# First batch of a fused graph kernel: one copy moved to ScalarE's queue, one message moved behind the distances, and a small addition moved from VectorE to GpSimd near the end

## The reference

```
h = relu(bn(conv1(x)));  x_conv = relu(bn(conv2_17taps(h)) + x)
s = x @ w_se.T + b_se                       # 3 numbers per node
A = exp(-(|s_n|^2 + |s_m|^2 - 2 s_n.s_m)) * adj
x_nmp = A @ relu(x @ w_msg.T + b_msg)
r, z, n = gates([x_conv, x_nmp] @ w_ih.T, x @ w_hh.T);  x = layernorm(x + (1-z)*n + z*x)
# per group g of the first 25 nodes:
A = adj_g + eye;  dinv = deg(A) ** -0.5
out_g = relu((dinv*A*dinv) @ relu((dinv*A*dinv) @ x @ W1[g] + b1[g]) @ W2[g] + b2[g])
```

## Time and profile before

| | |
|---|---|
| median of 3 runs | 357.75 us (356.75 to 357.86) |
| span of the profiled execution | 356.6 us |
| TensorE busy | 339.5 us, 95% |
| VectorE busy | 319.4 us, 90% |
| ScalarE busy | 236.8 us, 66% |
| GpSimd busy | 94.2 us, 26% |

### The profile page before, as it was taken

The page is one execution under the profiler, slowest core; times in us unless marked ns, Lnnn a source line. Parts: engine busy times, 40 slices in busy tenths (PEclk is TensorE's granted clock), DMA queues, the critical chain, the costliest instruction groups (busy, mean ns, idle before and its releaser), DMA issues. The chain is left out here.

```text
span 356.6 us, 6244 instructions
## 1 busy us (share of the span) xinstructions
PE 339.5 (95%) x1767; PEld 275.7 (77%) x1767; DVE 319.4 (90%) x566; ACT 236.8 (66%) x410; POOL 94.2 (26%) x153
## 2 busy tenths in 40 slices
PE   4989999999999999999999999999999999999891
PEld 1577678986889688977988688968897798866670
DVE  2989999999999999999999899999999999896636
ACT  4383665748856696748764885669684886976752
POOL 4750001604050503222050505040231306052123
PEclk9989999999999999999999999999999999999997
DMA  6914241514043222604161403412260415301101
GB/s 195 307 26 130 83 132 44 170 31 148 18 129 129 74 76 61 211 0 147 36 202 34 147 13 103 156 55 92 55 193 25 147 31 147 119 22 36 29 2 53
DMA packets 30950, 33.95 MB, mean 95 GB/s; under 512 B 4884, under 2 KB 18124, under 8 KB 30932
## 3 DMA queue, kind: packets, MB, share of 16 engines
q1 hardware_dynamic: 30166, 33.55, 31.3%
q10 hardware_dynamic: 766, 0.18, 0.2%
HBM read 24.85 MB, written 4.40 MB: 82 GB/s over the span
## 5 line engine op out<-in xcount | busy, mean ns | idle before, releaser
L1276 POOL TENSOR_TENSOR base<-mv,vscale 128x4 f32<-128x4 f32 x16 | 6.0, 373 | 234.9 <-DVE mv L1405 228.2
L685 PE MATMUL p_outer<-t_h,w_h 128*128 128x344 f32 x131 | 41.9, 337 | 0.0
L685 PE MATMUL p_outer<-t_h,w_l 128*128 128x344 f32 x131 | 40.8, 328 | 0.0
L1373 DVE TENSOR_TENSOR am<-am,adj 128x512 f32<-128x512 f32 x64 | 40.0, 686 | 0.0
L1539 DVE TENSOR_TENSOR am_l<-am,am_h 128x2048 fp32r<-128x2048 f32 x15 | 34.3, 2287 | 1.8 <-ACT am_h L1130 1.8
L685 PE MATMUL p_middle<-t_h,w_h 128*128 128x344 f32 x90 | 28.6, 329 | 0.0
L1130 ACT ACTIVATE am_h<-am 128x2048 fp32r<-128x2048 f32 x15 | 28.5, 1901 | 0.0
L685 PE MATMUL p_middle<-t_h,w_l 128*128 128x344 f32 x90 | 28.0, 322 | 0.0
L685 PEld LDWEIGHTS p_outer<-t_h,w_h 128*128 128x128 f32 x131 | 25.0, 194 | 2.4 <-ACT t_h L1002 0.7
L1108 ACT ACTIVATE yoo<-yn,nb,rs 128x128 f32<-128x128 f32 x63 | 25.8, 483 | 0.0
L685 PEld LDWEIGHTS p_outer<-t_h,w_l 128*128 128x128 f32 x131 | 25.2, 195 | 0.3
(11 more groups left out here) (387 smaller groups left out, 1019.4 us busy)
## 6 DMA issues: line engine op xcount, KB each, us to landing
adj<-adjT SPq DMA_DIRECT2D x64, 256.0 KB, 3.2
xpad<-xT SPq DMA_DIRECT2D x17, 256.0 KB, 2.9
out<-yoo SPq DMA_DIRECT2D x16, 256.0 KB, 2.3
crossed<-left SPq DMA_DIRECT2D x31, 48.0 KB
left<-left SPq DMA_DIRECT2D x30, 48.0 KB
right<-left SPq DMA_DIRECT2D x30, 48.0 KB
wc<-w_c SPq DMA_DIRECT2D x2, 384.0 KB, 6.6
wraw<-g_w SPq DMA_DIRECT2D x1, 640.0 KB
```

The lines of the kernel that those rows point to most:

```text
L685: return nc.tensor.matmul(out_, w, x, start=start, stop=stop, skip_group_check=True)
L1276: TT(base[:, 0:CH], mv[:, :, 1], vscale[:, 0:CH], ALU.mult)
L1373: TT(am[:, c, :], am[:, c, :], adj[:, c, :], ALU.mult).then_inc(s_am[c], 1)
```

## The change

Four things change. The copy to `crossed` is issued by ScalarE instead of SP, behind `middle_high`. Batch 1's message is made right behind the first distances, into `p_gi` instead of `ring[1]`. The addition of the identity to `ac` is made by GpSimd in step 14 instead of by VectorE in the first batch, and the degrees get their 1 when VectorE takes them out of PSUM. ScalarE waits for the new addition before it scales `ac`.

```
@@ GroupsAct.degree_factors
                 last.then_inc(s_diag, 1)
+                act.wait_ge(s_ac, 1)
                 for j in range(PAIRS):
                     last = nc.scalar.activation(ac[0:CC, j, :], ac[0:CC, j, :], ACT.Identity, scale=dinv[:, j:j + 1])
@@
-        FIRST_MSG = p_z
+        FIRST_MSG, SECOND_MSG = p_z, p_gi
@@ sync
             sp.wait_ge(s_left, 1)
-            sp.dma_start(full(crossed[0:KD, :]), full(left[32:32 + KD, :])).then_inc(s_right[0], 16)
             spread_factors(1)
@@ tensor, degrees
-                pe.wait_ge(s_ac, 1)
+                pe.wait_ge(s_acd, 32 * BLOCKS); pe.wait_ge(s_mt, 2)
@@ tensor, first
                 last.then_inc(s_d, 1)
+                msg(1, SECOND_MSG)
                 pe.wait_ge(s_t3h, 1); pe.wait_ge(s_whi, 1); pe.wait_ge(s_w0, 1)
                 stream(3, p_outer, s_t3l, 1, 1)
-                pe.wait_ge(s_e[1], 1)
-                msg(1, R_MSG)
                 pe.wait_ge(s_t12h, 1); pe.wait_ge(s_whi, 2); pe.wait_ge(s_w2, 1)
                 stream(1, p_middle, s_t12l, 1, 2)
                 pe.wait_ge(s_whi, 3); pe.wait_ge(s_v, 1)
                 stream(2, p_outer, s_t12l, 1, 3)
-                pe.wait_ge(s_m0, 1); pe.wait_ge(s_mt, 2)
+                pe.wait_ge(s_m0, 1); pe.wait_ge(s_e[1], 1)
@@ scalar, first
                 middle_high(o)
+                act.wait_ge(s_left, 1)
+                act.dma_start(full(crossed[0:KD, :]), full(left[32:32 + KD, :])).then_inc(s_right[0], 16)
                 act.wait_ge(s_mt, 1)
@@ gpsimd, step 14
                     TT(dinv[:], dg[:, 3, :], dg[:, 0, :], ALU.mult).then_inc(s_dinv, 1)
+                    pool.wait_ge(s_deg, 1)
+                    TT(ac[0:CC, :, :], ac[0:CC, :, :], cst[0:CC, C_ID:C_ID + CC].unsqueeze(1).broadcast_to([CC, PAIRS, CC]), ALU.add).then_inc(s_ac, 1)
@@ vector, first
-                msg_sum(z, 1, R_MSG)
+                msg_sum(z, 1, SECOND_MSG)
@@
-                dve.wait_ge(s_acd, 32 * BLOCKS)
-                TT(ac[0:CC, :, :], ac[0:CC, :, :], cst[0:CC, C_ID:C_ID + CC].unsqueeze(1).broadcast_to([CC, PAIRS, CC]), ALU.add).then_inc(s_ac, 1)
@@
-                CP(dg[:, 0, :], p_gi[0:CC, 0:PAIRS]).then_inc(s_dg, 1)
+                TS(dg[:, 0, :], p_gi[0:CC, 0:PAIRS], 1.0, None, ALU.add).then_inc(s_dg, 1)
```

## The result

The changed kernel takes **359.74 us** (median of 20 runs, 358.51 to 364.08) against 358.03 for the kernel before (20 runs, 356.75 to 362.80). The ratio is 1.0046, with a 95% interval of 1.0027 to 1.0066: some 1.65 us slower, between 1.0 and 2.4. The forecast was 359.4 us, 2.1 above the 357.3 taken for the kernel before, and slower. A repeat on another chip, of 12 runs against 29, gave 360.01 against 358.55 and a ratio of 1.0028 [0.9989, 1.0066]: the same direction, smaller, and not apart from 1 by itself. Six of the 20 runs of the kernel before and three of the changed one's were disturbed and took some 4 us more than the rest; most of them are left out of the ratio and none of the medians, which without all nine are 357.76 and 359.67.

What follows compares the result with a forecast made beforehand. TensorE, busy 95% of the span, was taken as the bound, VectorE close behind at 90%. -1.1 early, +1.75 late and +1.5 for one slow clock stretch gave +2.15; 357.3 + 2.1 = 359.4 us, range 356.0 to 361.2.

Steps and rivals of the forecast that it cites:

- -1.1 for the copy: First batch: the copy lands before the distances need it, so `stream(1)` starts at 24.65 instead of 25.75, 1.1 us gained.
- +1.5 for the clock: One of two new TensorE idle times, before `stream(1)` or in step 14, brings a slow clock stretch costing 1.5 us.
- A smaller term, taken as 0: First batch: taking the 1.04 us addition off VectorE gains 0 on the path, at most 1.04.
- The addition on GpSimd, +1.75: Step 14: GpSimd's 1.85 us addition holds VectorE's `y2`, so `stream(4)` starts 1.75 us later (bounds 0 and 2.6).
- The rival of a free addition: Step 14: GpSimd misses both VectorE gaps and runs beside `second_sums`; only -1.1 is left, 356.2 us; chance 0.26.
- I take about 3 us, 16.3: First batch: the small copy, alone on ScalarE's queue, takes about 3 us and lands at 16.3, ahead of 17.87.
- The third rival: First batch: the copy on ScalarE's queue lands no earlier, at 17.87 + 1.3 or later; 359.05 us, chance 0.07.
- The chain behind the copy: First batch: earlier distances, exponentials and `w1_h` remove VectorE's 0.97 us wait, so its `p_middle` read releases `stream(1)` at 24.65.
- if that happens again: Idle time before `stream(1)` again brings 3.4 us at clock 0.50, over `stream(1)` and `stream(2)`: up to 1.7, priced 1.5.
- the low stretch in this place costs nearly nothing: First batch, clock 0.50 from 20.2 to 23.6: `stream(1)` waits for VectorE's read anyway, so it costs 0.15 us, not 1.7.
- TensorE is the bound in this stretch: First batch: TensorE takes nothing from VectorE soon behind the removed addition, so the gain is taken as 0.

Runs made afterwards that it cites:

- the first look at before: The kernel before, unchanged, in its first profiled execution: a span of 356.6 us.
- the addition alone: The kernel before with only the addition of the identity moved to GpSimd in step 14: 359.30 us, ratio 0.9999.
- the loads behind: The changed kernel with four of SP's loads issued behind the factor copies: 359.64 us; with GpSimd's addition also held until `y2` is written: 358.04 us.
- the early half: The changed kernel with the addition back on VectorE in the first batch, degrees copied out as before: 358.53 us, ratio 1.0.
- the copy alone: The kernel before with only the copy to `crossed` issued by ScalarE: 358.75 us, ratio 1.0023.
- the message alone: The kernel before with only batch 1's message made behind the distances, into `p_gi`: 358.08 us, ratio 0.9990.
- the addition alone behind `y2`: The kernel before with only the addition moved to GpSimd, held until VectorE has written `y2`: 357.28 us, ratio 0.9992.
- the addition-behind-`y2` kernel: The changed kernel with GpSimd's addition held until VectorE has written `y2`: 358.05 us, ratio 0.9949.
- the fill: The changed kernel with the addition back on VectorE and a write-only GpSimd fill of `rows2` in its place: 359.91 us, ratio 1.0046.
- the second look at before: The kernel before, unchanged, profiled once more: 357.71 us, with a span of 355.9.
- the `y2` wait again: The changed kernel with GpSimd's addition held until `y2` is written, measured a second time: 358.65 us, ratio 1.0022.

## Why the prediction was right, and where it wasn't

The time (359.74 against 359.4) and the sign came out. Of the three large terms one is right. The other two, -1.1 for the copy and +1.5 for the clock, did not come and cancelled nearly, which was luck. A smaller term, taken as 0, was -0.35. That the level is closer than the difference (1.65 measured, 2.1 forecast) is luck as well: the kernel before had a median of 358.03 in its 20 runs, not 357.3.

**The addition on GpSimd, +1.75: mechanism right, size a little high.** 1.85 us was said for the instruction, 1.86 measured. VectorE's `yb` was held and not `y2`: GpSimd began 0.17 us ahead of it. `stream(4)` lost 1.35 us against the first look at before and 1.30 against the second; 1.43 with the addition alone. In the four traces that have the addition in this place the way to `stream(4)` is 253.75 to 253.83, in the ten others 252.23 to 252.45. How 1.75 comes down to 1.35 can be read off: `yb` was held for 2.25 - 0.69 = 1.56, it began 0.15 sooner behind batch 1's product than in the first look at before (300.73 - 51.51 = 249.22 against 301.64 - 52.27 = 249.37), and 0.06 of slack between the last sum and `stream(4)` was used up (0.11 before, 0.05 now): 1.56 - 0.15 - 0.06 = 1.35. It is shown from four sides: gone without the addition, there with it alone, gone behind `y2` in either kernel, gone with a fill in its place. The rival of a free addition needed GpSimd to miss the gap of 0.19 us ahead of `yb`. In the same four traces it never did, and began 0.16 to 0.17 us ahead of `yb`.

**The copy on ScalarE's queue, -1.1: failed**, at "I take about 3 us, 16.3". The third rival, at 0.07, was the true one. The distances started at 18.78 and 19.13 in the two traces of the changed kernel, at 19.17 and 18.14 in those of the kernel before: either queue lands in the same range, and so does a copy issued 2 us later (18.43 and 18.12 in the table). What sets it is the load that is under way; with four loads behind it, the copy was there before 17.91. That is one trace: in the other with the loads behind, TensorE came to the distances only at 18.99, too late to tell. The 7.1 us of `bmsg` was the right row to go by, and the 2.1 of `vec` the wrong one: `vec` was issued at 0.73, when 34 to 96 GB/s were moving in the next two microseconds, and `bmsg` at 3.36, when 311 to 353 were. The rule of the Trainium skill cited there (DMA: Bandwidth & Descriptors, "Queues, rings and completion order") speaks for this outcome, and the trace agrees with what it would give; whether completion order or shared bandwidth delayed the copy, the runs do not separate.

The chain behind the copy was read rightly, only its price was a little high. `stream(1)` follows the distances, and the product follows `stream(1)`, so an earlier copy is kept. But the sum let `stream(1)` start 0.02 us behind VectorE's read, where the rows have 0.15 (25.60 to 25.75). And where the copy was in time the read ended 6.81 us behind the start of the distances, not 6.43, since VectorE had no wait left to give up: 24.87 is 0.88 before the 25.75 of the first look, not 1.1. Of this the loads behind gave back 0.25 on the way to the product (26.43 against 26.18). With the copy as late as before, nothing is won: ratios of 1.0 for the early half, 1.0023 for the copy alone, 0.9990 for the message alone. The price was also worked out from an idle time of 1.30 that another execution of the same kernel had at 0.54.

**The low clock, +1.5: failed.** The idle time before `stream(1)` came as said (1.05 to 1.55; 1.32 to 1.41 in nine traces), though it is not the edit's alone: with the message where it was, the copy alone has 0.44, the addition alone behind `y2` 0.84 and the addition alone 1.39. The clock stayed at 1.00 behind it. In the addition-behind-`y2` kernel, with 1.41 us of idle time:

```profile
23.60:27.00 3.40, 1.99 (x13) 1.00 0.04 1
```

The same holds with the early half alone, the addition alone, the loads behind (both), the fill, the message alone, the repeat of the changed kernel and that of the `y2` wait: nine traces with 1.32 to 1.41 us. Behind the two idle times of step 14 it stayed at 1.00 too (in the changed kernel's profile):

```profile
303.40:306.80 3.40, 2.34 (x15) 1.00 0.30 91
```

The step was "if that happens again", taken from one row. The old place does not hold up as a rule either. Both looks at the kernel before had the low clock there, behind 1.30 and 0.54 us of idle time before the distances, and the first trace of the changed kernel behind 1.16; its repeat did not behind 1.08, and the fill kernel did not behind 1.42:

```profile
20.20:23.40 3.20, 3.20 (x24) 3.20 (x24) 2.11 (x3) 3.16 (x6) 2.76 (x2) 1.00 0.09 7
```

(Its engines' busy times stand ahead of the clock: PE, PEld, DVE, ACT, POOL.) That the low stretch in this place costs nearly nothing was right for two of the three: the changed kernel ran its message in 1.87 us instead of 1.16, and `stream(1)` still waited only for VectorE's read, which ended at 24.49 + 0.69 = 25.18. In the second look at before it cost 0.6 us, because the copy was early and the read was over before `stream(3)` and the message.

**The addition leaving the first batch, 0: it gained 0.35.** TensorE's wait for batch 1's message sum ahead of the product was 0.55 to 0.57 us in five traces with the addition on VectorE and 0.20 to 0.22 in six without it, and the way from `stream(1)` to the product was shorter by the same 0.35. The exceptions are the second look at before (0.22) and the two with the loads behind (0.44 and 0.74). "TensorE is the bound in this stretch" was the step that failed: the product, at the end of it, waits for VectorE. Most of the 1.04 us was lost on the way, 0.30 of it in a new wait of VectorE for the degrees, in the changed kernel:

```profile
38.32 0.17 DVE L1523 TENSOR_SCALAR dg<-p_gi 106x8 f32<-106x8 f32 x1 [0.30 <-PE p_gi L685]
```

**What the sum should have been:** 0 for the copy, -0.35 for the addition leaving the first batch, +1.35 to 1.43 for it on GpSimd, no clock: 1.0 to 1.1 above before. Measured were 1.65 (1.0 to 2.4), on the repeat 1.0 (-0.4 to 2.4), and with the addition alone 0.8 in the median and 1.25 in the lowest run. What is behind the rest, if there is one, is open. The way from `stream(4)` to the end is 0.2 longer than before in the changed kernel, but as long (52.14 to 52.18 against 51.93) with the early half, the copy or the addition alone and with the fill, so no one edit shows as its cause. Open too is whether any version beats the kernel before: 0.9949 and 0.9955 for two kernels with the `y2` wait stand against 1.0022 for the repeat of the first, and the addition alone behind `y2`, with a lower median and a ratio of 0.9992, lies between. None is shown to.

## What to carry to other kernels

An operation handed to an idle GpSimd is not free if it reads SBUF: it costs what VectorE's instructions with two SBUF inputs lose beside it, so tie its start by a semaphore to a stretch where VectorE reads PSUM. Here a second queue did not bring a small copy past the bulk loads under way; issuing the loads later did, at a price where the loads are wanted. Before an idle time or a low clock seen once is priced, look at a second execution of the same kernel, and compare intervals between two events that depend on each other, not starts: of the 0.76 us of early "gain" 0.43 came with the execution, and the 0.33 that the edit gave were hidden in it.

## What the runs showed of the hardware

- The granted clock fell to 0.50 late in the kernel in three of the 14 traces: with the `y2` wait again (338.6 to 348.7, above), with the message alone, and in the repeat of the changed kernel (us, PE busy, granted clock, DMA share, GB/s):

```profile
339.80:343.10 3.30, 3.30 (x18) 0.50 0.00 0
343.30:350.00 6.70, 6.18 (x44) 1.00 0.01 2
```

That execution has a span of 359.5 against 357.4 for the same code. From `stream(4)` of step 14 to the end these three take 56.50, 53.60 and 53.81 us, the others 51.4 to 52.2. So a part of the spread of runs is this.
- An issue of the same 48 KB copy takes 1.34 us on ScalarE and 0.92 on SP.
- Neither the length of an idle time nor the distances' 24 rows told whether the clock fell: 0.54 and 1.16 us did and 1.42 us did not, with the same instructions around them.
- Of a VectorE instruction with two SBUF inputs and a GpSimd one that reads SBUF, the second to begin was held: GpSimd 0.04 us ahead gave `left` 2.32 us and GpSimd 1.81 (the copy alone), VectorE 0.11 ahead gave 0.75 and 2.32.
